# Rotary attention with two head groups per accumulator bank, and a new step order in five stages

## The reference, cut to what matters

```python
NL, D, H, DFF = (6, 128, 16, 512)
HD = D // H
def _attn(q, k, v, mask):
    scores = jnp.einsum('bqhd,bkhd->bhqk', q, k) / np.float32(np.sqrt(HD))
    scores = jnp.where(mask[:, None, None, :], jnp.float32(-jnp.inf), scores)
    w = jax.nn.softmax(scores, axis=-1)
    return jnp.einsum('bhqk,bkhd->bqhd', w, v)
for i in range(NL):
    xn = _adaln(x, noise_emb, n1_w[i], n1_b[i])
    q, k, v = jnp.split(xn @ qkv_w[i].T, 3, axis=-1)
    q = _rope(q.reshape(B, L, H, HD)); k = _rope(k.reshape(B, L, H, HD))
    x = x + _attn(q, k, v, src_mask).reshape(B, L, D) @ so_w[i].T
    ...                                   # the same with the context's 77 keys
    h = jax.nn.gelu(xn @ f1_w[i].T + f1_b[i], approximate=False)
    x = x + (h @ f2_w[i].T + f2_b[i])
```

## Time and profile before

| quantity | value |
|---|---|
| median of 3 runs | 4515.62 us (4512.39 to 4520.6) |
| profiled execution | 4525.97 us |
| its span, first to last instruction | 4524.2 us |
| mean granted TensorE clock | 0.943 of 2.4 GHz |
| PE, DVE, ACT, POOL busy | 85%, 56%, 54%, 30% |
| stage 6 with the last block | about 2355 to 4524 us |

### The profile page before, as it was taken

The page is one execution under the profiler, slowest core; times in us unless marked ns, Lnnn a source line. Parts: engine busy times, 40 slices in busy tenths (PEclk is TensorE's granted clock), DMA queues, the critical chain, the costliest instruction groups (busy, mean ns, idle before and its releaser), DMA issues.

```text
span 4524.2 us, 59445 instructions
## 1 busy us (share of the span) xinstructions
PE 3858.0 (85%) x23545; PEld 1740.2 (38%) x23545; DVE 2549.8 (56%) x4960; ACT 2431.1 (54%) x3415; POOL 1365.5 (30%) x1349
## 2 busy tenths in 40 slices
PE   5589999999999988998775888888888888888886
PEld 4367433334763344334441233322322323323333
DVE  5632444543235435443548676677676777776764
ACT  3534554554345454544211776666666767667764
POOL 3500234333004402430313233332332432432311
PEclk9689999999999998998886999999999999999998
DMA  2000000000001010001001001111111110110100
GB/s 90 1 19 1 38 15 20 10 15 15 25 1 42 20 34 15 13 23 56 26 8 44 25 27 37 39 33 34 39 36 30 45 34 26 46 37 23 37 11 15
DMA packets 103830, 124.78 MB, mean 28 GB/s; under 512 B 25059, under 2 KB 88747, under 8 KB 101624
## 3 DMA queue, kind: packets, MB, share of 16 engines
q1 hardware_dynamic: 103552, 120.99, 8.8%
HBM read 58.00 MB, written 1.45 MB: 13 GB/s over the span
## 4 chain that ended last, share of the span: by engine, by line
PE 65%; DVE 19%; ACT 8%; POOL 4%; issue 2%; DMA 1%; SPq 0%; POOLq 0%; DVEq 0%; ACTq 0%
PE ps L1814 8%; PE ps L1629 6%; PE ps L1613 6%; PE ps L1533 5%; PE ps L1525 5%; DVE c1sm L2497 4%; PE ps L1741 3%; ACT wB L2040 3%; DVE c0sm L2497 3%; PE ps L1800 3%; PE ps L1768 2%; PE ps L1554 2%; PE ps L1661 2%; PE ps L1849 2%; PE ps L1857 2%
## 5 line engine op out<-in xcount | busy, mean ns | idle before, releaser
L2040 ACT ACTIVATE wB<-ps 128x1024 f32<-128x1024 f32 (+1 forms) x762 | 765.6, 1021 | 321.2 <-PE ps L1800 314.9
L2497 DVE TENSOR_REDUCE c1sm<-ps 128x2 f32<-128x1024 f32 x384 | 460.3, 1220 | 114.0 <-PE ps L1768 110.6
L2497 DVE TENSOR_REDUCE c0sm<-ps 128x2 f32<-128x1024 f32 x384 | 460.4, 1220 | 99.1 <-PE ps L1768 97.1
L2338 DVE TENSOR_REDUCE c1sm<-ps 128x2 f32<-128x1024 f32 x128 | 155.1, 1222 | 201.8 <-PE ps L1578 200.5
L2338 DVE TENSOR_REDUCE c0sm<-ps 128x2 f32<-128x1024 f32 x128 | 155.6, 1222 | 180.9 <-PE ps L1578 180.1
L2040 ACT ACTIVATE c0m<-ps 128x1024 f32<-128x1024 f32 (+1 forms) x198 | 202.3, 1022 | 73.3 <-PE ps L1800 71.5
L1814 PE MATMUL ps<-wB,c1ar 128*9 128x512 f32 x1204 | 204.8, 608 | 19.8 <-ACT wB L2040 12.2
L1814 PE MATMUL ps<-wB,c0ar 128*9 128x512 f32 x1248 | 210.7, 628 | 12.6 <-ACT wB L2040 9.8
L1800 PE MATMUL ps<-c0ar 64*128 64x512 bf16 (+1 forms) x864 | 169.5, 392 | 53.1 <-DVE c1sm L2497 25.0
L2669 POOL TENSOR_TENSOR c0m<-c0m 128x512 f32<-128x512 f32 (+1 forms) x78 | 96.9, 1242 | 379.5 <-DVE c0m L2486 306.0
L1800 PE MATMUL ps<-c1ar 64*128 64x512 bf16 (+1 forms) x864 | 167.8, 391 | 44.5 <-DVE c0sm L2497 16.7
(11 more groups left out here) (706 smaller groups left out, 8812.7 us busy)
## 6 DMA issues: line engine op xcount, KB each, us to landing
c0ar<-c0m SPq DMA_DIRECT2D x216, 128.0 KB, 2.5
c1ar<-c0m SPq DMA_DIRECT2D x216, 128.0 KB, 2.4
c0m<-rscr SPq DMA_DIRECT2D x96, 128.0 KB, 2.9
c1m<-rscr SPq DMA_DIRECT2D x96, 128.0 KB, 2.9
wA<-in_lay SPq DMA_DIRECT2D x6, 1346.0 KB, 5.8
wA<-in_w SPq DMA_DIRECT2D x1, 4248.0 KB, 21.7
wA<-in_w SPq DMA_DIRECT2D x1, 4104.0 KB, 12.3
wA<-in_w4b SPq DMA_DIRECT2D x1, 2948.0 KB, 9.4
```

The lines of the kernel that those rows point to most:

```text
L2040: e.activation(P.ap[0:n, :, :], u.ap[0:n, :].rearrange("p (a q) -> p a q", a=2), ACT.Exp, scale=S8).then_inc(*A(("P8", n0, s, k), free=[u]))
L2338: e.tensor_reduce(c.sm[:, 2 * (g % 2), 2 * j:2 * j + 2], u.ap.rearrange("p (h k) -> p h k", h=2)[:, :, 0:n], AX, ALU.max, negate=True).the ...
L2497: e.tensor_reduce(c.mneg[:, s // 4, j, :, s % 4], u.ap.rearrange("p (a k) -> p a k", a=2), AX, ALU.max, negate=True).then_inc(*V(free=[u]))
```

## The change

Two groups of four heads now share one accumulator bank. The values of a pair of heads are laid out in 27 columns: nine zeros, nine of the second head, nine of the first. An even group multiplies by columns 0 to 17, so it writes zeros on the first nine partitions and its own result on the next nine. The odd group multiplies by columns 18 to 26 and adds onto the first nine. The bank is opened at the first step of the even group and closed at the last of the odd one. So `oc`, `o8` and `norm` run twice for an attention and not four times; `norm` takes one reciprocal of twice the size and multiplies twice. The weights' columns are permuted on the host so that the values come out in this order.

```diff
-                if k == 0:
+                first, end = g % 2 == 0 and k == 0, g % 2 == 1 and k == nc_ - 1
+                if first:
                     (acc,), t = yield Want([("T", .97)], [banks.last], tp)
...
-                if k == nc_ - 1:
+                if end:
                     (o,), t = yield Want([("A", .6)], [G6], t[0])
-                    emit("oc", c, n0, g, acc, o)
+                    emit("oc", c, n0, g // 2, acc, o)
...
-            while len(over) < 4:
+            while len(over) < 2:
...
-                    h = 4 * g + i
-                    vv = VC[l % 2][0:n, c.i, h, :] if cross else c.V8[0:n, k, h, :]
-                    x = e.matmul(acc.ap[32 * i:32 * i + 9, :], vv, Ps[i // 2].ap[0:n, i % 2, :], start=first, stop=end,
-                                 skip_group_check=True)
+                    vv = VC[l % 2][0:n, c.i, 4 * (g // 2) + i, :] if cross else c.V8[0:n, k, 4 * (g // 2) + i, :]
+                    vv = vv[:, 18:27] if g % 2 else vv[:, 0:18]
+                    x = e.matmul(acc.ap[32 * i:32 * i + (9 if g % 2 else 18), :], vv, Ps[i // 2].ap[0:n, i % 2, :],
+                                 start=first, stop=end, skip_group_check=True)
...
             def t8(c, n0, n1, u, ao, zt):
-                w.wait_ge(*V.at(("ao", n0, 3)))
+                w.wait_ge(*V.at(("ao", n0, 1)))
+                w.wait_ge(*V.at(("ao", n0, 0)))
...
-                e.reciprocal(c.rc, ov[:, :, 8]).then_inc(*V())
+                e.reciprocal(c.rc.rearrange("p (x a) -> p a x", x=2), ov[:, :, 8:18:9]).then_inc(*V())
...
+                for y in range(2):
+                    i = e.tensor_tensor(v4(ao.ap)[:, :, 64 * g + 32 * y:64 * g + 32 * y + 32].rearrange("p j (i e) -> p j i e", i=4),
+                                        ov[:, :, 9 - 9 * y:17 - 9 * y].rearrange("p (j i) e -> p j i e", j=4),
+                                        c.rc[:, 16 - 16 * y:32 - 16 * y].rearrange("p (j i) -> p j i", j=4).unsqueeze(3)
+                                        .to_broadcast([128, 4, 4, 8]), ALU.mult)
+                i.then_inc(*V(("ao", n0, g), free=[u]))
```

The wider values need room (864 columns for 576, for each batch and each of two context buffers). It is taken from the areas from which `G6` is cut: the list had nine buffers of 512 columns and has six. `mk6` also zeroes the nine extra columns:

```diff
                 for c in six:
-                    e.tensor_copy(c.V8[:, :, :, 8], KM[:, c.i, :].unsqueeze(2).to_broadcast([128, 4, 16])).then_inc(*V())
+                    e.memset(c.V8[:, :, :, 0:9], 0.0).then_inc(*V())
+                    for y in range(2):
+                        e.tensor_copy(c.V8[:, :, :, 17 + 9 * y], KM[:, c.i, :].unsqueeze(2).to_broadcast([128, 4, 8])).then_inc(*V())
```

```diff
-    "6": dict(lag=0.1458, weight=0.0, even=0.0005, held=0.2113, table=1.4514, apart=62.8755, spread=0.0, seed=8180),
+    "6": dict(lag=0.1211, weight=0.0207, even=0.0006, held=0.2643, table=2.045, apart=54.6944, spread=0, seed=8027, bias=dict(T=0.244, S=0.373, VTA=-0.191, TVb=-0.010, A=-0.534, VG=-0.949, G=-0.159, TA=-0.046)),
...
+        self.kind = "".join(step[0] for step in chain) + ("b" if bulk else "")
...
                 key = e[0] + (self.even * x[3].work if x[3] else 0.0) + self.weight * (e[1][-1][2] if e[1] else 0.0)
+                key += self.bias.get(x[1].kind, 0.0)
...
+    def level(self, banks):
+        t = max(self.clock.values())
+        for k in self.clock:
+            self.clock[k] = t
+        for u in banks.use:
+            u.t = t
```

More of the change, by code:

```diff
@@ L21 @@
 ORDER = {
[L22 to L27, removed]
[L28 removed]
+    "0": dict(lag=0.25, weight=0.0041, even=0.0212, held=0.1956, table=1.9081, apart=0, spread=0.9602, seed=5709, bias=dict(A=-0.723, TVAV=0.185, TV=0.835, TVV=-0.294, VG=-0.166, V=-0.115, G=-0.777, TA=0.509)),
+    "1": dict(lag=0.242, weight=0.0005, even=0.0137, held=0.0101, table=1.6552, apart=60, spread=0.3838, seed=3649, bias=dict()),
+    "2": dict(lag=0.1343, weight=0.0781, even=0.0213, held=0.0425, table=2.1835, apart=52.1484, spread=0, seed=7013, bias=dict(S=-0.172)),
+    "3": dict(lag=0.3, weight=0, even=0.0154, held=0.05, table=3.0167, apart=0, spread=0, seed=1833, bias=dict(TA=0.436, T=-0.171, S=1.124, VG=-1.104, TVb=-0.406, TAV=0.479, TV=0.178)),
+    "4": dict(lag=0.0827, weight=0.1098, even=0.0092, held=0.0304, table=0.6638, apart=31.8048, spread=0, seed=9063, bias=dict(T=0.080, TVb=-0.117, VG=-0.156)),
+    "5": dict(lag=0.1, weight=0.0219, even=0, held=0, table=0.6, apart=29.3805, spread=0.2584, seed=4379, bias=dict(G=-0.325, TVA=-0.547, TAV=-0.111)),
+    "6": dict(lag=0.1211, weight=0.0207, even=0.0006, held=0.2643, table=2.045, apart=54.6944, spread=0, seed=8027, bias=dict(T=0.244, S=0.373, VTA=-0.191, TVb=-0.010, A=-0.534, VG=-0.949, G=-0.159, TA=-0.046)),
 }
@@ L479, in build, with heads2 @@
             f.zT, f.ring = Bufs([own(512)]), Bufs([own(512) for _ in range(4)])
-            f.T, f.sm = own(1536).rearrange("p (k q) -> p k q", k=3), own(24).rearrange("p (k n) -> p k n", k=6)
+            f.T, f.sm = own(1536).rearrange("p (k q) -> p k q", k=3), e.s7.rearrange("p (k n) -> p k n", k=6)
             last.append(f)
-        KC = [cos[k].ar[:, 9344:10576].bitcast(BF).rearrange("p (s b q) -> p s b q", s=8, b=NB) for k in range(2)]
-        KCf = [cos[k].ar[:, 9344:10576].bitcast(BF).rearrange("p (s q) -> p s q", s=8) for k in range(2)]
-        VC = [wA[0:NCTX, 2 * LCOLS + 1024 + 576 * k:2 * LCOLS + 1600 + 576 * k].rearrange("p (b h e) -> p b h e", b=NB, h=16)
+        KC = [cos[k].ar[:, 9056:10288].bitcast(BF).rearrange("p (s b q) -> p s b q", s=8, b=NB) for k in range(2)]
+        KCf = [cos[k].ar[:, 9056:10288].bitcast(BF).rearrange("p (s q) -> p s q", s=8) for k in range(2)]
+        VC = [wA[0:NCTX, 2 * LCOLS + 1024 + 864 * k:2 * LCOLS + 1888 + 864 * k].rearrange("p (b q r) -> p b q r", b=NB, q=8)
               for k in range(2)]
-        spare = [[wA[:, 0:WA_COLS], 2 * LCOLS + 2176], [wB, 0], [areas[0][:, 0:5632], 0], [areas[1][:, 0:5632], 0]]
+        def heads2(v):
+            return v[:, :, 9:27].rearrange("p q (y e) -> p q y e", y=2)[:, :, :, 0:8]
+        spare = [[wA[:, 0:WA_COLS], 2 * LCOLS + 2752], [wB, 0], [areas[0][:, 0:5632], 0], [areas[1][:, 0:5632], 0],
+                 [cos[0].ar, 10288], [cos[1].ar, 10288]]
         def carve(n):
@@ L1106, in norm @@
             def norm(g, o, t):
-                (u,), t = yield Want([("T", .6), ("V", .57)], [banks], t)
+                (u,), t = yield Want([("T", .6), ("V", .8)], [banks], t)
                 emit("o8", c, n0, g, u, ao, o)
@@ L1122, in attn6 @@
                     _, t = yield Want([("T", .97)], [], tp)
-                emit("a8", c, l, n0, g, k, n, [P for P, _ in ps], acc, vkeys, cross, k == 0, k == nc_ - 1)
+                emit("a8", c, l, n0, g, k, n, [P for P, _ in ps], acc, vkeys, cross, first, end)
                 for P, _ in ps:
                     P6.give(P, t[0])
-                if k == nc_ - 1:
+                if end:
                     (o,), t = yield Want([("A", .6)], [G6], t[0])
-                    emit("oc", c, n0, g, acc, o)
+                    emit("oc", c, n0, g // 2, acc, o)
                     banks.give(acc, t[0])
-                    plan.spawn(norm(g, o, t[0]), c)
-            while len(over) < 4:
+                    plan.spawn(norm(g // 2, o, t[0]), c)
+            while len(over) < 2:
                 yield
@@ L1281, in build @@
         fence("0")
+        plan.level(banks)
         emit("load", "w2", "wB", "0")
@@ L2831, in arrays_of @@
     twin = np.array([(2 * s + p) * 8 + (dd + 4) % 8 for p in range(2) for dd in range(8) for s in range(8)])
+    turn = np.array([(8 * q + 4 * y + i) * 8 + dd for q in range(2) for i in range(4) for y in range(2) for dd in range(8)])
     both = lambda w: np.concatenate([w[:, perm], w[:, twin]], axis=1)
```

31 lines of the change are left out of this document (16 added, 15 removed).

## The result

| | before | after |
|---|---|---|
| median | 4518.11 us | 4324.89 us (4322.08 to 4332.43, 4 runs) |
| ratio, 95% interval | | 0.9576 [0.9559, 0.9593] |
| profiled span | 4524.2 us | 4330.6 us |
| stage 6 begins (last mask instruction) | 2356 us | 2333 us |
| stage 6 and last block | 2168 us | 1998 us |

The forecast had the sign and missed the size: -193 us and not -46. Of the 193, 170 lie in stage 6 and 23 ahead of it (in other profiled executions with the same orders ahead of stage 6 that border stood between 2318 and 2333 us).

A forecast was written before the change was run, and what follows sets the result against it. No engine full in stage 6, TensorE first suspect. Stage 6 -42 for removed rounds +2 for wider weights = -40 us, other stages -6, sum -46: from 4515.62 to 4470 us, range 4436 to 4504.

The forecast's parts named there:

- What bounds the kernel: Stage 6: no engine full, TensorE first suspect (83% busy), its gaps waits for banks VectorE or ScalarE still reads.
- What goes: Stage 6, 96 of 192 rounds removed: 57 us of TensorE, 63 us of ScalarE, 24 us of VectorE.
- What of it is on the path: Stage 6: how much removed work comes back as time; 42 us taken.
- The three readings: Stage 6 gain: half the chain's direct count, 21 us; chain shares, 47; TensorE bounds and gaps scale, 69.
- The other stages: Ahead of stage 6, same instructions in a new order: -6 us, with +12 and -25 as ends.
- Rival 1: All stages: TensorE bounds throughout and order improves, -82 us, 4434 us; sign: its body share rises from 83%; chance 0.17.
- Rival 2: Stage 6: the wait moves to maxima and exponentials, TensorE idles instead; -13 us, 4502 us; chance 0.15 together with Rival 4.
- Rival 3: Stage 6: scratch buffers run short, +29 us, 4545 us; sign: evictions wait for transposes, norms for output projection; chance 0.06.
- Rival 4: Stage 6 body: thinner work lowers the clock from 0.96 to 0.93, 4502 us; chance 0.15 together with Rival 2.

The follow-up runs named there:

- e9: Kernel before, order untouched, second and fourth round of each attention made small (fewer columns evicted, one transpose of four, no reciprocal): 4516.06 us, 0.9998.
- e1: Changed kernel with all weights of ORDER as before and no offsets, planner's clocks still levelled: 4578.93 us, 1.0124.
- e6: e1 with one offset added in stage 6, T=0.244 (sums over keys chosen later): 4522.01 us, 0.9997.
- e5: Kernel before with levelled clocks and one offset in stage 6, T=0.244 (sums over keys chosen later): 4499.85 us, 0.9954.
- e2: Kernel before, four rounds for each attention, with the new ORDER weights, offsets and levelled clocks: 4460.62 us, 0.9868.
- e3: Changed kernel with the old ORDER weights in stage 6 alone and no offsets there: 4558.23 us, 1.0068.
- e4: Changed kernel with all eight offsets taken out of stage 6, its other new weights kept: 4664.15 us, 1.0317.
- e7: Changed kernel without the stage 6 offset T=0.244 (sums over keys later), the other seven kept: 4592.42 us, 1.0157.

## Why the prediction was wrong

- **What bounds the kernel.** "No engine is full" was right, and so was where: stage 6. I wrote that each TensorE gap is a wait for a bank that VectorE or ScalarE still reads, and that was wrong: of its 279 idle us between 2400 and 4150, 39 are waits of the sums for exponentials, and 40 are waits of the maxima's transposes (L1790) for their operand from VectorE (L2512). The idle time in the loads of L1814 was in view, and I asked nothing of it, since I looked for what the removed steps cost.
- **What goes.** Counts and prices held: 384 multiplies fewer, 18-column loads at 96 ns, table loads 26 and 24. The reciprocal was off (350 ns). TensorE's busy time fell by 94 us and not by 57 to 66: about 19 us of stage 6 are other multiplies that took less time, and 13 us lie ahead of it.
- **What of it is on the path: failed.** This is the step of the 42 us. The three readings (21, 47, 69 us) assume that removed time comes back by its share of the chain, in whatever order. At the old order nearly the same work is worth 0 (e9); with the old weights and the new structure the time rises by 56 us (e1), where I had -40; with T in both it rises by 19 us (e6 against e5); with the full new weights it falls by 132 us (changed kernel against e2). One number for the worth of the rounds doesn't exist. In the new order doing them twice costs 90 us, twice my 42, though that prices work added, and taking work away from that order wasn't tried.
- **The other stages: sized too small, inside the bounds.** -6 forecast, 23 to 25 us measured (e3 against e1), at the far end of the range that I gave. From the first multiplies of each stage, stage 0 gives 11 us (experts begin at 237 for 248 us), stages 1 to 3 about 7 more, stage 4 about 7 more.
- **The order of stage 6: the missing term.** I gave the whole new order -6 us, all of it outside stage 6, and in stage 6 counted the edit as if the order were kept, a term put at nothing without a reason. The same structure runs at 4325, 4558 and 4664 us by row "6" alone. The order alone, on the old structure, is worth 60 us (e2). Neither half alone gives what both do: -60 us from the order, +56 from the structure, -193 together. The likely reason is that the new weights were chosen for the new structure, but nothing here shows it: weights and offsets chosen afresh for four rounds weren't tried. They might reach below the 4461 us of e2, and then less of the 132 us would be the structure's.
- **The rivals.** Rival 1 had the direction (4434 us) and not the size, and its sign came, TensorE's share of the body rising. Rival 2 has a parallel in e1 alone, where the idle time grew by more than the work that went; but its price was a gain of 13 us, and e1 lost 56. Rival 3, the scratch buffers: six suffice in the new order, at least for 4325 us. Its sign, evictions that wait for transposes, has no row in the waits of e1 or of the changed kernel. Since the planner counts the buffers, a shortage can lie in the order instead, and how much of e1's loss is theirs wasn't tried. Rival 4 went the other way: the body's granted clock rose, from 0.96 to 0.97. The windows 2400 to 4150 us of e4 and of the changed kernel:

```profile
2400.00:4150.00 1750.00, 1413.61 (x9387) 479.84 (x9387) 1143.62 (x1723) 1027.17 (x1202) 542.66 (x648) 0.89 0.11 31
```

```profile
2400.00:4150.00 1750.00, 1534.15 (x11232) 551.93 (x11232) 1356.16 (x2084) 1220.11 (x1436) 636.47 (x757) 0.98 0.13 37
```

The slow order issues 9387 multiplies in 1750 us at a granted clock of 0.89, the fast one 11232 at 0.98. Both programs have the same 23161 multiplies, so their totals can be split. Of the 337 us between the two profiled executions, 189 are TensorE's idle time and 148 its busy time (3912.8 and 3764.4 us). For e7 the split of 258 us is 160 and 98. So about two fifths of what these orders cost lies in multiplies that take longer, beside a lower granted clock (0.910 and 0.921 over the whole program, 0.945 in the changed kernel). The clock doesn't simply follow the stalls: T took 65 us of idle time out of e1 (e6) while the clock fell from 0.928 to 0.920 and the busy time rose by 11 us. e5 shows the same against the kernel before: 40 us less idle, 11 us more busy, 0.943 to 0.937.

**What stays open.** That placing the sums later carries most of what the eight offsets give in the changed kernel is shown: without it alone 263 us are lost (e7), without all eight 335 (e4). Why is not. The exponentials' wait at the sums is not the main cause: the multiplies lost 29 us there in e7, and halving the exponentials in the old order brought 35 us. The distance by itself is not it either: it grew as far in e5 and brought 21 us. What goes with T in the sweep is TensorE's wait for the reductions of the maxima (153 to 65 us) and the clock. My guess is that sums placed later also let the scores go first that feed VectorE and ScalarE. The trace agrees in kind (VectorE is busy 1356 of 1750 us after, 1197 in e7), but no run tests it, since each engine's busy time in a window rises with the speed whatever the cause.

## What to carry to other kernels

Where engines work in a fixed order and none is full, ask first for whom the busiest engine waits, and read it from the waits of its multiplies, not of its weight loads: the loads' 101 us here were 39 us of TensorE. Where the consumer stands behind the producer in the order is worth trying, but what it gives depends on the rest of the order: the same offset was worth 263 us in the changed kernel, 57 in e1's, and 21 in the kernel before (with the levelled clocks). Value an edit at a fixed order before counting on it: make the work small, or do it twice, and see whether the time moves. A structure and its order must be timed together, since here either half alone would have misled: one gave a third of the gain, the other a loss.

## What the runs showed of the hardware

A weight load grew from 89 to 96 ns when its columns went from 9 to 18, while the multiplies of the changed kernel took 606 ns with 18 and 602 ns with 9 on average. A reciprocal of 32 columns out of PSUM took 350 ns for 251 with 16. The granted clock between 2400 and 4150 us differed by the order of the same instructions alone, from 0.89 (e4) to 0.98 (changed kernel).
